# Attention on one core: one run of scores and maxima per step, with a ring of four PSUM banks

## What is computed

```
x_h = layernorm(x) as (b, 16 heads, 512, 16)
xw  = einsum('bhtd,hde->bhte', x_h, w_att_val)
att = softmax(einsum('bhte,bhse->bhts', xw, x_h) / sqrt(16))
vx  = layernorm(x) @ wv_w.T + wv_b
x   = x + (att @ vx) @ out_w.T + out_b
x   = x + ffn(layernorm(x))      # fp4-quantized gate, up, down
```

## Time and profile before

| | us |
|---|---|
| median of 3 runs | 1658.5 (1653.16 to 1659.29) |
| the profiled execution | 1653.08, span 1651.3 |
| attention, from the first maxima to the last projection | 66.1 to 1084.0 of the span |
| busy over the span: PE, DVE, ACT, POOL | 1533.3 (93%), 1340.0 (81%), 852.9 (52%), 525.0 (32%) |

### The profile page before, as it was taken

How to read it: one execution, slowest core, us unless ns; L and a number is a source line. 1 busy time by engine, 2 the same in 40 slices (tenths; PEclk the granted TensorE clock), 3 DMA queues, 4 the chain that set the end, 5 groups by cost and what they waited for, 6 DMA issues and landing times. The chain is left out here.

```text
span 1651.3 us, 33543 instructions
## 1 busy us (share of the span) xinstructions
PE 1533.3 (93%) x8874; PEld 866.6 (52%) x8874; DVE 1340.0 (81%) x2731; ACT 852.9 (52%) x1714; POOL 525.0 (32%) x676
## 2 busy tenths in 40 slices
PE   3389999999999999999999999869999999999998
PEld 3134544544544544544544544336666766666666
DVE  7487787787787787787787777369999999999996
ACT  2156666666666666666666666623333333333332
POOL 2214314314314314314314312023444333444332
PEclk8589999999999999999999999989999999999999
DMA  4524344344344344344344333000000000000000
GB/s 161 155 73 124 105 116 117 104 115 117 104 115 117 104 116 117 104 116 117 104 115 117 104 104 124 11 1 14 16 16 16 16 16 13 16 16 16 16 16 19
DMA packets 82531, 127.34 MB, mean 77 GB/s; under 512 B 28864, under 2 KB 48448, under 8 KB 82368
## 3 DMA queue, kind: packets, MB, share of 16 engines
q1 hardware_dynamic: 74720, 119.55, 25.5%
q10 hardware_dynamic: 7776, 7.36, 1.4%
HBM read 81.67 MB, written 45.15 MB: 77 GB/s over the span
## 5 line engine op out<-in xcount | busy, mean ns | idle before, releaser
L1002 DVE TENSOR_REDUCE neg_max<-max_bank 128x1 f32<-128x512 f32 x1024 | 666.9, 683 | 189.8 <-PE max_bank L804 180.2
L941 ACT ACTIVATE probs<-scores 128x512 f32<-128x512 f32 x1024 | 555.8, 595 | 351.0 <-PE scores L818 347.3
L1343 PE MATMUL gu_bank<-splits,f_x_T 128*128 128x352 f32 x1024 | 315.6, 461 | 2.1 <-ACT f_x_T L1321 2.1
L815 PE MATMUL scores<-q_stack,x_stack 64*128 64x512 f32 x1024 | 256.1, 497 | 21.3 <-ACT probs L941 21.1
L830 PE MATMUL pv<-probs,v_quad 128*32 128x512 f32 x2048 | 272.7, 605 | 1.2 <-ACT probs L941 1.2
L815 PEld LDWEIGHTS scores<-q_stack,x_stack 64*128 64x128 f32 x1024 | 95.8, 183 | 299.3 <-ACT probs L941 269.2
L1343 PEld LDWEIGHTS gu_bank<-splits,f_x_T 128*128 128x128 f32 x1024 | 190.6, 191 | 98.4 <-ACT f_x_T L1321 2.7
L804 PE MATMUL max_bank<-x_stack,q_stack 64*128 64x512 f32 x1024 | 209.9, 406 | 27.1 <-DMA x_stack<-x_split 15.0
L818 PE MATMUL scores<-max_stack,max_ones 64*128 64x512 f32 x1024 | 203.3, 393 | 0.0
L1171 POOL TENSOR_TENSOR f_rstd<-f_mean_var,eps 128x1 f32<-128x1 f32 x64 | 44.7, 699 | 382.6 <-DVE f_mean_var L1281 382.6
L1361 PE MATMUL y_bank<-splits,h_T 128*128 128x256 f32 x640 | 148.9, 380 | 1.1 <-ACT h_T L1301 1.1
(11 more groups left out here) (128 smaller groups left out, 2004.9 us busy)
## 6 DMA issues: line engine op xcount, KB each, us to landing
q_stack<-q_split SPq DMA_DIRECT2D x512, 64.0 KB, 2.4
x_stack<-x_split SPq DMA_DIRECT2D x256, 128.0 KB, 2.7
x_split<-splits SPq DMA_DIRECT2D x64, 256.0 KB, 2.2
q_split<-splits SPq DMA_DIRECT2D x64, 256.0 KB, 2.3
out_dram<-x_all SPq DMA_DIRECT2D x64, 128.0 KB, 1.7
x_all<-in_L_attn_x_dram ACTq DMA_DIRECT2D x14, 512.0 KB, 5.0
max_rows<-max_turned SPq DMA_DIRECT2D x256, 4.0 KB, 1.8
max_stack<-max_rows SPq DMA_DIRECT2D x128, 8.0 KB
```

The source lines that it names most:

```text
L815: pe.matmul(scores[banks[m][0]][:, :], row_tile(x_stack[g], m)[:, p, j * P:(j + 1) * P], row_tile(q_stack[g], m)[:, p, :], start=True, sto ...
L941: act.activation(probs[j % 2][:, h, :], scores[bank_of(g, QUAD * j + h)[0]][:, :], ACT.Exp).then_inc(p_ready, 1)
L1002: dve.tensor_reduce(neg_max[g % 2][:, at:at + 1], max_bank[bank_of(g, k)[0]][:, :], AX.X, ALU.max, negate=True).then_inc(m_used, 1)
L1343: m = pe.matmul(gu_bank[c][:, :], x_T[u][:, a, :], gate_up_T[:, a, c * CH:(c + 1) * CH], start=(a == 0), stop=(a == HALVES - 1))
```

## The change

PSUM is cut another way: four banks for scores (one for each head of a step), and a ring of four banks that maxima, values and other work share in the fixed order `TILES_IN_RING`. Each tile waits until the tile four places before it has been emptied (`room`).

PE's order in a step is now: scores pair 0, maxima pair, scores pair 1, maxima pair, and only then one group of another shape: at j = 0 the second half (steps 2 and 3) of the values of the quad before, at j = 2 the first half (steps 0 and 1) of this quad, and at j = 1 and 3 one to three pieces of other work. `probs` has four buffers instead of two.

The two halves of the values are summed apart: ACT copies each (`begin_half`, `end_half`, after the four exponentials of the step), so once more per quad than before, and POOL adds them (`add_halves`). POOL's work of a batch is in the order `POOL_STEP`. DVE does its other work after the four reductions of a step instead of between them.

The core of the diff:

```diff
-    probs = [sb(f"probs{u}", [P, QUAD, T]) for u in range(2)]
+    probs = [sb(f"probs{j}", [P, QUAD, T]) for j in range(TT)]
+    pv_more = sb("pv_more", [P, T])
...
-    scores = [pb(f"scores{k}", [P, T]) for k in range(3)]
-    max_bank = [pb(f"max_bank{k}", [P, T]) for k in range(3)]
-    pv = pb("pv", [P, T])
-    misc = pb("misc", [P, T])
+    scores = [pb(f"scores{k}", [P, T]) for k in range(QUAD)]
+    ring = [pb(f"ring{k}", [P, T]) for k in range(4)]
...
-    IN_STEP = {(0, 0): "x0", (0, 1): "q0", (0, 2): "rows3", (0, 3): "turn0",
-               (1, 0): "turn1", (1, 1): "proj0", (1, 2): "rows0", (1, 3): "proj1",
-               (2, 0): "x1", (2, 1): "q1", (2, 2): "rows1", (2, 3): "v0",
-               (3, 0): "v1", (3, 2): "rows2"}
+    IN_STEP = {(0, 1): ("x0",), (0, 3): ("rows3", "q0"), (1, 1): ("turn0", "rows0"), (1, 3): ("turn1",),
+               (2, 1): ("proj0", "x1"), (2, 3): ("q1", "v0", "rows1"), (3, 1): ("proj1",), (3, 3): ("rows2", "v1")}
...
+    TILES_IN_RING = []
+    for g in range(QUADS):
+        for j in range(TT):
+            TILES_IN_RING += [("max", g, QUAD * j + k) for k in range(QUAD)]
+            if j % 2 == 0:
+                TILES_IN_RING.append(("pv", g, j // 2))
+            else:
+                TILES_IN_RING += IN_STEP[g, j]
+    TILES_IN_RING += [None] * (-len(TILES_IN_RING) % len(ring))
...
-    STATS = [(0, 3), (1, 0), (1, 1), (1, 2)]
-    AGGREGATE = (1, 3)
+    STATS = [(0, 1), (1, 0), (1, 2), (2, 0)]
+    AGGREGATE = (2, 1)
+
+    POOL_STEP = {(0, 0): ("values",), (0, 1): ("halves", "x0"), (0, 3): ("q0",),
+                 (1, 0): ("values",), (1, 1): ("halves",),
+                 (2, 0): ("values",), (2, 1): ("halves", "x1"), (2, 2): ("deviation",), (2, 3): ("q1",),
+                 (3, 0): ("normal0", "values"), (3, 1): ("halves", "normal1"), (3, 2): ("normal2",),
+                 (3, 3): ("normal3",)}
...
+            def add_halves(i, g):
+
+                pool.wait_ge(pv_begun, i + 1)
+                pool.wait_ge(pv_ended, i + 1)
+                pool.tensor_tensor(pv_rows[g % 2][:, :], pv_more[:, :], pv_rows[g % 2][:, :], ALU.add)\
+                    .then_inc(pv_summed, 1)
...
-                    for p in range(PAIRS):
-                        key_scores(i, g, j, p, start)
-                        if ahead:
-                            max_scores(i + 2, ab, ag, PAIRS * j + p, False)
-                        if p == 0 and j > 0:
-                            weigh_values(i, b, g, j - 1, start)
-                        elif p == 0 and not start:
-                            weigh_values(i - 1, b - (g == 0), (g - 1) % QUADS, TT - 1, False)
-                    if stands(kind, b):
-                        for half in range(2):
-                            other(half, kind, b)
+                    for p in range(PAIRS):
+                        key_scores(i, g, j, p, start)
+                        if ahead:
+                            max_scores(b, g, PAIRS * j + p)
+                    if j == 0 and not start:
+                        weigh_values(b, g, True)
+                    if j == 2:
+                        weigh_values(b, g, False)
+                    for kind in IN_STEP.get((g, j), ()):
+                        if stands(kind, b):
+                            other(kind, b)
```

More of the change, by code:

```diff
@@ L709, in batch @@
[L709 to L710 removed]
+                for g in range(QUADS):
+                    for j in range(TT):
+                        for task in POOL_STEP.get((g, j), ()):
+                            if task == "values":
+                                ready_values(b, g, first)
+                            elif task == "halves":
+                                if not (first and g == 0):
+                                    add_halves(QUADS * b + g - 1, (g - 1) % QUADS)
+                            elif task == "deviation":
+                                if prepared(b + 2):
+                                    deviation(b + 2)
+                            elif task[:6] == "normal":
+                                if prepared(b + 2):
+                                    normalize(b + 2, int(task[6]))
+                            elif prepared(b + 1):
+                                split(task, b)
@@ L810, in key_scores @@
-                banks = [bank_of(g, k) for k in at]
-                free = [k - bank[1] + 1 for k, bank in zip(at, banks) if not (start and k < 3)]
-                if free:
-                    pe.wait_ge(p_ready, QUAD * TT * i + max(free))
+                if not (start and j == 0):
+                    pe.wait_ge(p_ready, QUAD * (TT * i + j - 1) + ROWS * p + ROWS)
                 for m in range(ROWS):
-                    pe.matmul(scores[banks[m][0]][:, :], row_tile(x_stack[g], m)[:, p, j * P:(j + 1) * P],
+                    pe.matmul(scores[ROWS * p + m][:, :], row_tile(x_stack[g], m)[:, p, j * P:(j + 1) * P],
@@ new lines, in prepare @@
+                    for half in range(2):
+                        s = 2 * a + half
+                        terms = [(xs, w, n) for xs, w in ((xl, vw_low), (xl, vw_high), (xh, vw_low), (xh, vw_high))
+                                 for n in range(HALVES)]
+                        for k, (xs, w, n) in enumerate(terms):
+                            m = pe.matmul(out[:, half * E:(half + 1) * E], xs[:, n, s * P:(s + 1) * P], w[:, n, :],
+                                          start=(k == 0), stop=(k == len(terms) - 1))
@@ L882, in other @@
-                    for s in range(2 * half, 2 * half + 2):
-                        m = pe.transpose(misc[:, s * P:(s + 1) * P], o_rows[:, s, a * P:(a + 1) * P],
+                    if a == 0:
+                        pe.wait_ge(sum_used, uses_before(b, BY_DVE))
+                    else:
+                        pe.wait_ge(sum_used, use("rows3", b, BY_DVE) + 1)
+                    for s in range(TT):
+                        m = pe.transpose(out[:, s * P:(s + 1) * P], o_rows[:, s, a * P:(a + 1) * P],
@@ new lines, in finish, with other @@
+                    for half in range(2):
+                        t = 2 * a + half
+                        for n in range(HALVES):
+                            m = pe.matmul(out[:, half * E:(half + 1) * E], o_T[n][:, t * P:(t + 1) * P],
+                                          out_T[:, n, :], start=(n == 0), stop=(n == HALVES - 1))
+                m.then_inc(misc_ready, 1)
+            def other(kind, b):
+                for semaphore, count in room([kind], b):
+                    pe.wait_ge(semaphore, count)
+                if kind in PREPARE:
+                    prepare(kind, b + 1)
+                else:
+                    finish(kind, b)
@@ L1113, in _ @@
             for kind in ("rows3", "proj0", "proj1"):
-                for part in range(2):
-                    other(part, kind, B)
+                other(kind, B)
 def ffn_block(nc, ctx, x_all, ident, minus_half, eps, gate_up_T, down_T, out):
```

346 lines of the change are left out of this document (175 added, 171 removed).

## The result

The changed kernel takes 1786.6 us (median of 4 runs, 1785.5 to 1788.5), beside 1658.2 us for the kernel before: a ratio of 1.078, 95% interval 1.076 to 1.081. The forecast was 1750 with a range up to 1780: the side was right, the time is 37 us beyond the forecast and beyond the range.

A forecast was written before the change was run, and what follows sets the result against it. PE was taken to bound the kernel; a batch would go from 61.9 to 60.0 + 4.3 + 3.4 + 1.7 = 69.4 us, in all +98 on 1653.1: 1750 us, range 1690 to 1780.

The forecast's parts named there:

- Terms 1 and 2: PE per batch: 14 fewer shape interruptions, 2.8 us off; values of two steps in one shape, 0.8 us off.
- Terms 3 to 5: PE per batch: waits for POOL and ACT go, 1.1 and 1.2 us off; ring adds 2.7, short steps 1.3: 60.0.
- term 4: Group after each run waits for DVE to reduce the run's first maximum: 16 x 0.17 = 2.7 us.
- Term 6: First scores of quad 2: maxima arrive late through SP's 17.2 us chain behind q0; PE stands 4.3 us a batch.
- Term 7: Second maxima of (3, 0): v0 waits for POOL to spread quad 3's values; PE loses 3.4 us a batch.
- Term 8: Half clock behind PE's stop at quad 2: 1.7 us a batch, bounds 0 and 3.6.
- The clock stays high: Rival: the clock does not fall at PE's stops, 1727 us; chance 0.27 (1705 to 1735).
- Faster: Rival: SP's chain is shorter than quad 1 and values are spread in time, 1619 us; chance 0.07.
- One stop absent: Rival: one of PE's two stops is absent or half as long, 1665 to 1720 us; chance 0.13.
- The runs do not close up: Rival: each run's second pair finds its bank late, 0.2 lost per step, 1795 us; chance 0.08 (worse than 1780).

The follow-up runs named there:

- Experiment 6: Changed kernel with x0 and q0 moved to (0, 0) and (0, 2), quad 3's values spread in (2, 0), x stacks loaded before q's store lands: 1622.9 us.
- Experiment 2: Changed kernel with x0 moved to step (0, 0) and q0 to (0, 2): 1715.6 us.
- experiment 5: Changed kernel with PE filling its two stops by 14 and 10 pairs of unread matmuls on both row halves: 1714.5 us.
- experiment 9: Experiment 6 with x0 back in step (0, 1): 1613.9 us.
- experiment 7: Changed kernel with x0 and q0 early, quad 3's values spread early, and each run ordered maxima, scores, maxima, scores: 1637.3 us.
- experiment 8: Experiment 6 with each run ordered maxima, scores, maxima, scores: 1615.0 us.
- experiment 10: Experiment 8 with x0 back in step (0, 1): 1615.4 us.
- experiment 4: Changed kernel with PE filling its two stops by 14 and 10 unread matmuls on one half of the rows: 1741.4 us.

## Why the prediction was right and where it was wrong

**Terms 1 and 2 were right.** The groups are 0.23 apart, and the fused values take 1.85, where I had 0.24 and 1.87.

**Terms 3 to 5, and their sum of 60.0, were 1.1 too high.** Experiment 6 shows a batch without stops: 60.16. It contains what the earlier q0 costs in quad 0 and step (1, 0), 14.72 (627.38 to 642.10) - 14.10 and 4.29 (to 646.39) - 3.69 (669.87 to 673.56 in the changed kernel): 1.2 us. The changed kernel's own figure is then 58.9: without the stops the new order is faster than before, as the sum said too. The waits did take the form of term 4, the group behind the run for `neg_max` (0.22 in the row above, 1.88 after the run's start, where I had 1.77). Part of the 1.1 us too many is that pieces of other work now follow one another: v0 behind q1 takes 1.89 (632.01 to 633.90) where the earlier trace rows have 2.08, and rows1 behind it 0.53 where term 7 has 0.59. The rest I can't give to single terms.

**Term 6 was right.** I had a chain of 17.2 us and a stop of 4.3; the trace has 17.1 and 4.28. Experiment 2 starts the chain earlier, experiment 6 shortens it, and the stop goes with it.

**Term 7 was right.** I had 3.1 us before the second maxima of (3, 0), released by `o_rows`, and 0.3 behind; the trace has 3.24, released by `o_rows`. Step (3, 0) and the one behind it are 5.96 us longer than in experiment 6 (634.43 to 643.39 to 647.74 against 612.01 to 615.69 to 619.36), of which 2.4 are the clock (experiment 5): 3.5 for the stop with what it leaves.

**Term 8 is the step that failed, by its size.** I put 1.7 us a batch, with 3.6 as the upper bound; experiment 5 measures 4.9, beyond the bound. Three parts of it failed:

- That the clock falls only at the longer stop. I took the 3.1 us of the earlier trace rows as the time PE must stand. At the second stop it fell after 2.4.
- That it stays low for 3.8 us of work. It was some 6 at both stops. From the first scores behind the first stop to the next run PE took 6.23 us where experiment 5, with the clock high, has 3.67: 2.6 us. With the 2.4 at the second stop these are the 4.9; I had 1.7 for one. The 3.8 were also too few for the earlier trace rows themselves: between their two windows PE worked another 0.69 us, at 1091.23, while the clock was low.
- That the earlier trace rows bounds it: one fall of the clock, in another stage, was used as if it were a constant. In the changed kernel itself it isn't one. In batch 1 the stops were as long as in the others, but the low stretches were half as long, and this batch took 69.5 us (187.52 to 257.02), about what I had forecast. From the first stop to the next run it took 4.98 (187.52 to 192.50) instead of 6.23; then its second stop, with windows:

```profile
187.52 0.65 PE L873 MATMUL scores<-q_stack,x_stack 64*128 64x512 f32 x2 [4.54 <-DMA max_stack<-max_rows]
...
192.50 0.50 PE L873 MATMUL scores<-q_stack,x_stack 64*128 64x512 f32 x2
...
210.14 0.50 PE L865 MATMUL ring<-x_stack,q_stack 64*128 64x512 f32 x2 [3.24 <-DVE o_rows L1121]
...
257.02 0.79 PE L873 MATMUL scores<-q_stack,x_stack 64*128 64x512 f32 x2 [4.11 <-DMA max_stack<-max_rows]
```

```profile
209.00:210.00 1.00, 0.00 (x0) 0.00 (x0) 0.97 (x3) 0.00 (x0) 0.00 (x0) 1.00 0.00 0
...
211.00:212.00 1.00, 1.00 (x12) 0.35 (x8) 1.00 (x4) 0.00 (x0) 0.00 (x0) 0.80 0.46 131
...
215.00:216.00 1.00, 0.93 (x8) 0.40 (x6) 0.72 (x2) 1.00 (x3) 1.00 (x2) 0.99 0.60 193
```

Here the clock was still high when PE went on at 210.14. It fell at 211.6, with PE at work for 1.5 us, and was high again at 215.0: low for 3.4 us instead of 6.8. At the first stop it fell at 187.7, 0.2 us after PE had gone on. The next batch is 71.5 us long (257.02 to 328.49), and the rest are 71.5 to 71.9. In experiment 2, where only the second stop is left for the clock, the time from it to the next run goes up and down between 3.7 and 4.3 from batch to batch. So the same stop can cost more or less in clock, and its length doesn't say which.

In the Trainium skill, "TensorE: Matmul & The Clock Gate", section "HAM oscillation" describes a kernel that waits for a transfer in every round and therefore starts every round at the low clock. This trace agrees for the first stop, the one for a transfer: the clock fell at it in every batch. It fell as well at the second, where PE waits for DVE.

**The sum.** 58.9 (for 60.0) + 4.3 + 3.5 (for 3.4) + 4.9 (for 1.7) = 71.6, and 71.58 was measured. This is no independent check, since the 58.9 and the 3.5 come from differences of the same steps; for the 58.9 experiment 9 is one: its 59.57 less the 0.6 that step (1, 0) still takes too long are 59.0. Over the twelve periods the error of 2.2 us makes 26 of the 37. Of the other 11, four are the same error in two more batches; and I gave batch 0 four microseconds for all, while it has both stops (4.42 at 118.04 and, at 140.56, 3.31). What exactly the rest is was not followed up.

**The rivals.** "The clock stays high" (1727) fell, and experiment 5, which makes it true, gives 1714. "Faster" fell, since both stops are there. "One stop absent" is true of no kernel here by itself; made true, it gives 1689 and 1716, within the 1665 to 1720 that I gave. "The runs do not close up" fell with the distances of 0.23; its 1795 is near the time that was measured, for another reason.

## What to carry to other kernels

When a reordering moves the start of a long chain of stores and loads, or of one item in an in-order queue, follow that chain to the one who needs its end: here the new order cost 8%, and was 2.2% faster than the kernel before (1.9 to 2.5) once q0 with its x0, one task of POOL and four loads were moved to the front. Count a stall of PE twice, once for its length and once for the half clock behind it, and take the second from several stretches of the profile or as a wide range: one fall read from another stage gave 1.7 us where these two cost 2.6 and 2.4. A gain on a waiting engine that only moves the wait to the next operand (experiments 7, 8 and 10) should be forecast at nothing until the next operand is named.

## What the runs showed of the hardware

- The clock fell 2.4 us after PE's last instruction in one stop and 3.4 us after it in another of the same batch, and was low for 6.8 us both times, some 6 us of it with PE at work. In batch 1 it fell only after PE had gone on (0.2 and 1.5 us after, 4.7 us after PE's last instruction before the stop) and was low for 3.4 us both times. In the earlier trace rows it fell after 3.1.
- In experiment 4 the clock fell at 616.0 after 2.56 us of matmuls on one half of the rows and an idle time of 0.74, with PE at work again since 615.26. In batch 0 of that run it fell at 117.6, in the middle of such matmuls (115.18 to 119.05), 3.6 us after PE's last instruction before them. In experiment 5, with pairs on both halves and 0.21 idle, it did not. Nor did it fall in experiment 4 at the second stop of the first three batches (2.5 us from there to the next run, in the later ones 3.9 to 4.2). Whether the half-used array or the gap decides was not separated.
- Sixteen matmuls of 128*32 in a row take 1.85 us, and twice the eight in a row would be 1.98: 0.13 is saved where they follow one another in one shape.
